# The first weights' load ahead of the second half of x, and the second half's row statistics behind the low parts of the first half

## What is computed

```python
def _layernorm(x, axis=-1, eps=1e-05):
    m = jnp.mean(x, axis=axis, keepdims=True)
    v = jnp.var(x, axis=axis, keepdims=True)
    return (x - m) / jnp.sqrt(v + eps)

x = x + _L0_xattn_ref(_layernorm(x, axis=-1), ctx_512, L0_xattn_Wq, L0_xattn_w_kc_q, L0_xattn_w_kc_kv,
                      L0_xattn_W_qr, L0_xattn_W_kr, L0_xattn_Wo)
x = x + _L0_ffn_ref(_layernorm(x, axis=-1), L0_ffn_w_fc, L0_ffn_w_proj)
```

## Time and profile before

| | |
|---|---|
| median of 3 runs | 393.04 us |
| lowest and highest | 392.11 and 395.31 us |
| profiled execution, its own time | 395.22 us |
| its span, first to last instruction | 393.0 us |
| TensorE clock granted, mean | 0.987 of full speed |
| busy: PE, DVE, ACT, POOL | 368.8, 298.2, 208.3, 179.3 us |

### The profile page before, as it was taken

The page is one execution under the profiler, slowest core; times in us unless marked ns, Lnnn a source line. Parts: engine busy times, 40 slices in busy tenths (PEclk is TensorE's granted clock), DMA queues, the critical chain, the costliest instruction groups (busy, mean ns, idle before and its releaser), DMA issues.

```text
span 393.0 us, 6335 instructions
## 1 busy us (share of the span) xinstructions
PE 368.8 (94%) x2160; PEld 264.9 (67%) x2160; DVE 298.2 (76%) x675; ACT 208.3 (53%) x557; POOL 179.3 (46%) x170
## 2 busy tenths in 40 slices
PE   7899999999999999999999999987989778999996
PEld 6775676677666766776666787753356455778885
DVE  5796698699666986796779575587986967898663
ACT  1424576557655765676556693526953343573150
POOL 2443765466546654765566412754901042055100
PEclk9899999999999999999999999999989989999999
DMA  7539200200302002000021001200000000000001
GB/s 244 203 109 307 88 1 2 107 3 1 109 0 96 13 2 108 3 0 2 0 83 66 3 0 36 82 1 2 0 3 0 0 2 0 1 0 2 28 28 53
DMA packets 9086, 17.53 MB, mean 45 GB/s; under 512 B 2144, under 2 KB 6944, under 8 KB 8160
## 3 DMA queue, kind: packets, MB, share of 16 engines
q1 hardware_dynamic: 9056, 17.14, 12.9%
HBM read 16.09 MB, written 1.05 MB: 44 GB/s over the span
## 4 chain that ended last, share of the span: by engine, by line
PE 71%; DVE 16%; ACT 5%; POOL 3%; issue 2%; DMA 2%; SPq 0%; DVEq 0%
PE bank L1520 16%; PE bank L1591 8%; PE bank L1566 7%; PE bank L1582 6%; PE bank L1612 6%; PE bank L1550 4%; PE bank L1535 3%; PE bank L1828 3%; PE bank L1472 3%; DVE relu L1154 2%; PE bank L1439 2%; DMA blobs<-in_blob 2%; PE bank L1440 1%; PE bank L1441 1%; PE bank L1479 1%
## 5 line engine op out<-in xcount | busy, mean ns | idle before, releaser
L459 POOL TENSOR_TENSOR prob<-prob,rinv 128x512 f32<-128x512 f32 x64 | 65.9, 1040 | 74.4 <-DVE rinv L1024 74.4
L1520 PE MATMUL bank<-xnT,w 128*128 128x512 f32 x288 | 90.3, 434 | 1.5 <-DVE xnT L922 1.5
L620 ACT ACTIVATE prob<-bank,negmax 128x256 f32<-128x256 f32 x128 | 59.0, 478 | 29.6 <-DVE negmax L1018 29.6
L1018 DVE TENSOR_REDUCE negmax<-bank 128x2 f32<-128x512 f32 x64 | 40.9, 681 | 36.4 <-PE bank L1566 36.4
L1520 PEld LDWEIGHTS bank<-xnT,w 128*128 128x128 f32 x288 | 50.3, 189 | 19.4 <-issue 13.2
L630 ACT COPY probT<-bank 128x512 f32<-128x512 f32 x64 | 37.7, 588 | 22.9 <-PE bank L1582 22.9
L953 DVE TENSOR_TENSOR rot_up<-bank,cb 64x512 f32<-64x512 f32 x64 | 44.1, 689 | 1.6
L454 POOL TENSOR_TENSOR rot_low<-rot_low,rot_up 128x512 f32<-128x512 f32 x32 | 41.0, 1280 | 5.3 <-DVE rot_up L953 5.3
L1582 PE MATMUL bank<-ca,prob 128*128 128x128 f32 x256 | 39.3, 276 | 0.5 <-ACT probT L630 0.3
L439 POOL TENSOR_TENSOR c_y<-c_ve,minus_half 128x4 f32<-128x4 f32 (+1 forms) x9 | 9.8, 1086 | 64.2 <-DVE c_ve L903 48.6
L1582 PEld LDWEIGHTS bank<-ca,prob 128*128 128x128 f32 x256 | 29.2, 141 | 13.8 <-issue 5.3
(11 more groups left out here) (206 smaller groups left out, 706.1 us busy)
## 6 DMA issues: line engine op xcount, KB each, us to landing
blobs<-in_blob SPq DMA_DIRECT2D x7, 1024.0 KB, 4.8
xs<-in_x SPq DMA_DIRECT2D x2, 512.0 KB, 4.1
xn<-in_w_fc_t SPq DMA_DIRECT2D x1, 1024.0 KB, 4.9
ctxT<-in_w_proj_t SPq DMA_DIRECT2D x1, 1024.0 KB, 5.5
out<-qk SPq DMA_DIRECT2D x8, 128.0 KB, 1.7
cb<-in_const_b SPq DMA_DIRECT2D x1, 768.0 KB, 9.1
blobs<-in_w_gate SPq DMA_DIRECT2D x1, 704.0 KB, 4.4
blobs<-in_w_up SPq DMA_DIRECT2D x1, 704.0 KB, 5.8
```

The costliest lines, as they stand in the source:

```text
L459: pool.tensor_tensor(p[:], p[:], rinv[:, n % PROBS, :].unsqueeze(2).to_broadcast([P, 2, S]), ALU.mult).then_inc(normed, 1)
L620: ins = act.activation(prob[n % PROBS][:, st, :], pS[n % UNITS][:, st * S:(st + 1) * S], ACT.Exp, bias=negmax[:, n % UNITS, st:st + 1], ac ...
L1018: dve.tensor_reduce(negmax[:, n % UNITS, :], pS[n % UNITS][:].rearrange("p (a s) -> p a s", a=2), AX, ALU.max, negate=True).then_inc(max_r ...
L1520: ins = pe.matmul(q_bank(m)[:], w[a][:, k, r * P:(r + 1) * P], x[b][:, k, c * CH:(c + 1) * CH], start=(i == 0), stop=(i == 5))
```

## The change

SP issues the first weights and the identity matrix ahead of the second half of x. DVE takes the row statistics of the second half behind `turned_low(0)` and `turned_low(1)` instead of at its start; `rope(0)` now comes behind these statistics and ahead of the second half's Newton step and `negmean`; `rope(1)` comes ahead of `turned_low(2)` and `turned_low(3)`. PE runs `latent_q(2)` right behind `latent_q(1)`. `WARM` is 18 instead of 24. All work is the same apart from the six fewer warm-up matmuls.

```diff
--- before.py
+++ after.py
@@ -40,7 +40,7 @@
 MASKED = -1.5e38
 OUT_BANK = (0, 7, 2, 1)
 PREPS = 3
-WARM = 24
+WARM = 18
 UNITS = 4
 PROBS = UNITS
 SCORE_BANK = (1, 3, 5, 6)
@@ -378,9 +378,9 @@
         def _(sp):
             x_v = x.rearrange("(t p) d -> p t d", p=P)
             sp.dma_start(xs[:, 0:4, :], x_v[:, 0:4, :]).then_inc(d_x, 16)
+            sp.dma_start(wb[0][:, 0:C_KCKV], blob[0][:, 0:C_KCKV]).then_inc(d_first, 16)
+            sp.dma_start(ident, const_a[:, 0:A_CN]).then_inc(d_id, 16)
             sp.dma_start(xs[:, 4:8, :], x_v[:, 4:8, :]).then_inc(d_x2, 16)
-            sp.dma_start(ident, const_a[:, 0:A_CN]).then_inc(d_id, 16)
-            sp.dma_start(wb[0][:, 0:C_KCKV], blob[0][:, 0:C_KCKV]).then_inc(d_first, 16)
             sp.dma_start(cb[:], const_b).then_inc(d_cb, 16)
             sp.dma_start(wb[0][:, C_KCKV:BLOB], blob[0][:, C_KCKV:BLOB]).then_inc(d_blob[0], 16)
             sp.dma_start(ca[:, A_CN:CA], const_a[:, A_CN:CA]).then_inc(d_ca, 16)
@@ -961,12 +961,15 @@
                 rope_crossed(m, 0)
                 rope_crossed(m, DC)
 
-            for i in range(2):
+            def row_statistics(i):
+
                 dve.wait_ge((d_x, d_x2)[i], 16)
                 for t in range(4 * i, 4 * i + 4):
                     ins = dve.bn_stats(stats[:, t, :], xs[:, t, :])
                 in_order(ins)
                 aggregate(i + 1, 4 * i, 4 * i + 4)
+
+            row_statistics(0)
             newton(1, rstd, 0, 4)
             for t in range(4):
                 normalise(t).then_inc(norm_ready, 1)
@@ -974,14 +977,15 @@
                 w1_low(0, i)
             for i in range(2):
                 turned_low(i)
+            row_statistics(1)
+            dve.wait_ge(d_cb, 16)
+            rope(0)
             newton(2, rstd, 4, NT)
             dve.scalar_tensor_tensor(out=negmean[:, 4:NT], in0=mv[:, 4:NT, 0], scalar=-1.0, in1=rstd[:, 4:NT],
                                      op0=ALU.mult, op1=ALU.mult).then_inc(shift_ready, 1)
-            dve.wait_ge(d_cb, 16)
-            rope(0)
+            rope(1)
             for i in range(2, 4):
                 turned_low(i)
-            rope(1)
             rope(2)
             w1_low(1, 0)
             rope(3)
@@ -1642,9 +1646,9 @@
             turn(0, lambda t: xn[:, t, :], norm_ready, 0, (0, 1))
             latent_q(0)
             latent_q(1)
+            latent_q(2)
             prep(0, 2)
             turn(0, lambda t: xn[:, t, :], norm_ready, 0, (2, 3))
-            latent_q(2)
             prep(0, 3)
             prep(1, 0)
             for m in range(RT, QSTEPS):
```

## The result

The changed kernel takes 399.88 us in the median of 4 runs (399.04 to 400.55), against 393.01 us (4 runs, 392.11 to 395.31) for the kernel before: a ratio of 1.0164, 95% interval 1.0115 to 1.0214. It is slower by 6.9 us. On another chip (last experiment) it was 398.42 against 392.07, ratio 1.0172 (1.0119 to 1.0225). The forecast was 395.1 with a range up to 397.0 and most of the chance on a difference within 1%; the side was right, the size and the range were not.

What follows compares the result with a forecast made beforehand. PE was taken to bound the kernel (busy 368.8 of 393.0 us), the start of latent_q(3) deciding the end. DVE series 1.5 plus clock 0.6 made 2.1 us, 393.04 to 395.1; own range 394.2 to 396.0, full range 391.6 to 397.0.

Steps and rivals of the forecast that it cites:

- the series on DVE: Second-half statistics, rope(0), Newton step with negmean run in turn behind the low parts; shift_ready 18.7 instead of 17.23, 1.5 us later.
- the floor of 11.9: First half's low parts: if the weights come early, x normalised at 9.45 plus 1.14 and 1.34 sets the earliest end.
- the term for the clock: Half-clock stretch of 3.4 us near PE's gap at 18.0 to 20.8: costs 0.6 us, bounds nothing and 1.7.
- The same steps, 6.6 us: From shift_ready to latent_q(3) the steps stay as before (17.23 to 23.83), which puts latent_q(3) at 25.3.
- the sum: Whole kernel: 1.5 plus 0.6 gives 2.1 us slower, the median going from 393.04 to 395.1.
- latent_q(2) costed at nothing: PE: it ran while the second half was copied and split, so moving it up saves nothing.
- full clock for the folds and transposes: First half on PE: eight folds and eight transposes take 2.9 us, up to 11.3, against 4.03 at half clock.
- the baseline: Profiled execution of before, 395.22 us, lies 2.2 above the median 393.04; the added 2.1 was applied to that median.
- My 2.7: First half's low parts done at 12.7 instead of 15.37, 2.7 us earlier.
- The warm-up: Start of PE: six calls fewer end it 1.7 us earlier, at about 6.2, and cost nothing.
- Weights land no earlier: Rival: first weights still land at 9.95, folds and transposes run at half clock, 397.8 us; chance 0.09.
- Half clock in both places: Rival: half clock also under the first half's folds, low parts at 13.8, 1.1 us more, 396.2; chance 0.12.

Runs made afterwards that it cites:

- last experiment: The changed kernel again, no edit, for a second profile and more executions: 398.42 us, ratio 1.0172 to the kernel before.
- experiment 4: Changed kernel plus 15 matmuls of ones on PE while it waits for the second half of x: 396.81 us, ratio 1.0119 to the kernel before.
- experiment 11: Changed kernel with latent_q(2) back behind the transposes of the second half: 396.35 us, ratio 1.0109 to the kernel before.
- experiment 3: Changed kernel with the DVE order of before; load order, latent_q(2) and WARM as changed: 398.47 us, ratio 1.0159 to the kernel before.
- experiment 7: Changed kernel with rope(0) behind the second Newton step and negmean: 396.94 us, ratio 1.0093 to the kernel before.
- experiment 10: Changed kernel with rope(0) behind negmean and rope(1) behind the last low parts; statistics stay moved: 395.6 us, ratio 1.008 to the kernel before.
- Experiment 8: Kernel before with the new load order, second-half statistics right behind the first half's normalising, 8 matmuls of ones before latent_q(0): 394.23 us, ratio 1.001.
- the second profile of before: The kernel before, run again with no edit: 391.91 us, ratio 0.9949 to the same program's executions beside it.
- experiment 9: Kernel before with WARM 18 instead of 24, nothing else: 393.22 us against 392.07, ratio 1.0039.
- experiment 1: Kernel before with only the load order of the change: 396.61 us, ratio 1.0116 to the kernel before.

## Why the prediction failed

**Right: the series on DVE.** `shift_ready` at 18.7 was forecast and 18.26 measured; `latent_q(3)` at 25.3 plus 0.6, measured 26.0. That it fits to 0.1 us is in part luck: single terms missed and made up for each other, and of the clock 1.2 us lay ahead of `latent_q(3)` where 0.6 was put. The low parts were done at 11.8, not 12.7: the weights landed at 6.35 instead of 8.35, early enough that they no longer mattered, and the first half's normalising (8.10 to 9.48) was the limit, as the floor of 11.9 had said. `rope(0)` did wait, 0.7 us for `latent_q(0)`, which ran at half clock (2.38 us; 1.5 at full clock). POOL's rotation was beside the Newton step again (0.64, 0.40, 0.39, with 0.17 for the last).

**Wrong: the size of the term for the clock.** I put 0.6 us, with 1.7 as the bound, for one stretch of 3.4 us. It was 6.8 us long and reached over `latent_q(3)` to `latent_q(5)`, pure path work: `prep(0, 3)` and `prep(1, 0)` took 1.11 and 1.62 instead of 0.68 and 0.89, the three products 5.86 instead of 4.09, together 2.9. Experiments 4 and 11 measure the same 2.8 to 2.9 as the difference to this profile. In the second profile of the changed kernel the stretch began earlier and cost about 2.1. "The same steps, 6.6 us" stopped at the start of `latent_q(3)`, and the sum took the rest as unchanged; that was the gap in it. The page "TensorE: Matmul & The Clock Gate" of the Trainium skill, section Why this matters for your kernels, names a long idle gap between bursts of matmuls as what brings the clock down. The trace agrees that the clock fell behind idle time, but no single gap here was longer than 1.6 us; it was several short ones, with PE busy half of the time. In experiment 11 one gap was 1.9 us and no drop followed.

**Wrong: latent_q(2) costed at nothing.** On DVE's path its place does not matter, as experiment 11 shows (`negmean` 18.3, low parts done 22.8). But it was work that PE had while it waited. I named the gap and the clock two paragraphs later and did not join the two.

**Overlooked: a stretch under the first products.** In six of the nine profiles with the weights early (the changed kernel's first and experiments 3, 4, 7, 10 and 11) the clock fell between 11.3 and 12.6 us, in or just behind a wait of PE for DVE; of the five with the old load order only the first profile of before had one near there, at 10.7, behind its wait for the weights. I took full clock for the folds and transposes, which was right, and didn't ask about the waits behind them. In the first profile the stretch cost 0.7 us on the path and in experiment 10 more. Experiment 8, with 8 matmuls of ones in that wait, had no stretch, but it differs in other things too, so the cause isn't isolated.

**Wrong: the baseline.** The profiled execution of before was taken as its normal start plus 2.2 us of noise spread anywhere. Its noise sat in the very stretch that the change edits: late weights, half clock under the folds, POOL beside the Newton step. The second profile had its scores at 32.71. Against that start the change costs 5.2 to 6.6 us (37.91 and 39.32), not the 2.1 of the sum: what leads up to the last low parts gives 3.1 to 3.7 of it (they are done at 22.05 and 22.7 instead of 19.0) and the clock behind them 2.1 to 2.9. The first half had only 1.0 us to give there (low parts 12.8 to 11.8): in the second profile DVE came to the low parts at 10.45, when its normalising was done, and not when the weights allowed it; the two moves together bring that to 9.48. My 2.7 was the first profile's.

**The warm-up.** Costed at nothing; 1.2 us in the medians of experiment 9, not clear of the measurement. In the changed kernel even 18 calls ended at 7.52, not at 6.2 to 6.6 (PE began 6 or 7 records in each us until about 6 us, where the first profile of before had gone over to 11 at about 4), and were the last thing the folds waited for, behind weights at 6.35.

**Open.** In the medians the loss is 6.3 to 6.9 us. The start accounts for 5.2 to 6.6 us between the second profile of before and the two of the changed kernel, and for 3.9 between the first two. The loss in the medians fits the second profile of before as the usual start, but no run shows how often each start occurs. From the scores to the end, the profiles took 355.7 to 358.8 us, in step with how much half clock lay between 270 and 325 us (3.4, 6.8 or 10.2 us in all). Before and changed both show 357.6 among these; no run tells whether the change shifts how often each occurs.

Of the rivals, none was it. "Weights land no earlier" came nearest in size (397.8) with the wrong cause: they landed at 6.35. "Half clock in both places" put the first stretch under the folds, which ran at full clock; two stretches there were, but the one behind the gap was twice as long as I had priced it. No version here beats before clearly; experiment 8 equals it.

## What to carry to other kernels

Before a change to a stretch of a few us is costed, take that stretch from more than one execution, or ask which of its rows (a landing, a clock, a contention) are likely to be unusual; noise there is not spread over the kernel but is the baseline itself. Work moved out of a wait of PE isn't free just because the wait remains: without it the clock may fall for the work behind. And an early transfer is worth only the distance to the next thing that is waited for (here 1.0 us, of the 2.7 that the chain seemed to offer), while what is pushed behind it (statistics that had filled the wait) comes back on the path in full.

## What the runs showed of the hardware

The landing of one load scatters from execution to execution: the first weights, fourth in the queue, were there between 8.7 and 9.95 us in five profiles of the old load order, and second in the queue between 6.2 and 6.8 us in nine of the new one. The second half of x, now fourth, landed at 8.7 in experiment 1 and at 9.7 in experiment 3, in the same load order. TensorE's granted clock fell in stretches of 3.4, 6.8 or 10.2 us. PE at 2.35 busy of 4.7 us was followed by 6.8 us at 0.51; at 3.14 of 4.9 (experiment 11) or 4.70 of 4.7 (experiment 4) it was not. I had expected the short length only, from the one stretch in the start of the first profile. The small operations of the Newton step on DVE took 0.16 us each alone, and most of them 0.38 to 0.66 beside POOL's rotation of the context, in both kernels.
